# One-hot matrices of the first graph made on GpSimd, one behind each gather, in place of VectorE

## What is computed

```python
def _L0_gnn_ref(x, W, M, edge_src, edge_dst):
    self_term = x @ W
    msg = x @ M
    agg = jax.ops.segment_sum(msg[edge_src], edge_dst, num_segments=x.shape[0])
    return jax.nn.relu(self_term + agg)
...
x = x + _L0_gnn_ref(_layernorm(x, axis=-1), L0_gnn_W, L0_gnn_M, src, dst)
x = x + _L0_ffn_ref(_layernorm(x, axis=-1)[None], ...)[0]
```

## Time and profile before

| | us |
|---|---|
| median of 3 executions | 4055.15 |
| lowest, highest | 4053.32, 4062.95 |
| the profiled execution's own time | 4024.76 |
| its span, first to last instruction | 4023.5 |
| first gather of the visits starts | 63.84 |
| last gather of the visits starts | 2525.18 |

### The profile page before, as it was taken

The page is one execution under the profiler, slowest core; times in us unless marked ns, Lnnn a source line. Parts: engine busy times, 40 slices in busy tenths (PEclk is TensorE's granted clock), DMA queues, the critical chain, the costliest instruction groups (busy, mean ns, idle before and its releaser), DMA issues. The chain is left out here.

```text
span 4023.5 us, 43371 instructions
## 1 busy us (share of the span) xinstructions
PE 2676.5 (67%) x13459; PEld 1995.0 (50%) x13459; DVE 2157.3 (54%) x5820; ACT 903.1 (22%) x1563; POOL 2164.3 (54%) x2248
## 2 busy tenths in 40 slices
PE   2567867776677776877877877622694646555844
PEld 1344545554455455555555555401683535454844
DVE  6777667776655556554545555200263534344866
ACT  3001111111122221111111111100352423233633
POOL 4666666666666665666666666577014353534031
PEclk9767879898888888999899888755896867777978
DMA  9676656666666665666666666401221111111146
GB/s 298 207 253 189 195 182 201 202 195 190 191 202 198 194 191 173 206 204 199 209 195 208 209 202 194 112 13 14 64 70 27 45 27 32 39 26 36 44 138 203
DMA packets 476804, 601.22 MB, mean 149 GB/s; under 512 B 72486, under 2 KB 415390, under 8 KB 474526
## 3 DMA queue, kind: packets, MB, share of 16 engines
q1 hardware_dynamic: 378766, 375.94, 28.6%
q0 software_dynamic: 97216, 219.88, 20.0%
q10 hardware_dynamic: 592, 2.64, 0.2%
HBM read 313.06 MB, written 286.79 MB: 149 GB/s over the span
## 5 line engine op out<-in xcount | busy, mean ns | idle before, releaser
L1703 POOL DMA_INDIRECT ring<-xn_d,srci x1611 | 1567.2, 973 | 902.1 <-DVE ring L818 416.9
L1505 PE MATMUL wide<-ring,one_hot 128*128 128x256 f32 x3222 | 983.1, 442 | 470.5 <-DVE ring L818 351.7
L818 DVE SCALAR_TENSOR_TENSOR ring<-ring,same_v,wide 128x256 f32<-128x256 f32 x1610 | 770.3, 478 | 942.6 <-remote 405.9
L1505 PEld LDWEIGHTS wide<-ring,one_hot 128*128 128x128 f32 x3222 | 666.5, 218 | 740.8 <-DVE ring L818 318.4
L1611 PE MATMUL wide<-tab_parts,low_hot 128*128 128x208 bf16 x6288 | 659.9, 262 | 329.5 <-issue 308.7
L1737 POOL DMA_INDIRECT g<-tab_d,srt x500 | 480.8, 962 | 629.5 <-DMA sum_d<-g 480.4
L1611 PEld LDWEIGHTS wide<-tab_parts,low_hot 128*128 128x128 bf16 x6288 | 576.3, 100 | 413.2 <-issue 377.0
L1563 PE MATMUL wide<-w2s,hh 128*128 128x256 f32 x1568 | 424.8, 420 | 150.5 <-issue 88.5
L1563 PEld LDWEIGHTS wide<-w2s,hh 128*128 128x128 f32 x1568 | 335.5, 216 | 225.9 <-issue 102.8
L1553 PE MATMUL wide<-xt,w1s 128*128 128x512 f32 (+1 forms) x832 | 419.1, 631 | 41.2 <-ACT hh L1238 23.5
L1238 ACT ACTIVATE hh<-wide,b1c 128x512 f32<-128x512 f32 (+1 forms) x208 | 137.7, 663 | 1299.1 <-remote 627.3
(11 more groups left out here) (369 smaller groups left out, 1730.2 us busy)
## 6 DMA issues: line engine op xcount, KB each, us to landing
run_d<-ring SPq DMA_DIRECT2D x201, 1024.0 KB
ring<-xn_d,srci POOLq DMA_INDIRECT x1611
y_d<-yo SPq DMA_DIRECT2D x196, 128.0 KB
comb<-y_d SPq DMA_DIRECT2D x28, 896.0 KB, 10.5
low_row<-low_d SPq DMA_DIRECT2D x13, 1024.0 KB
sum_d<-g SPq DMA_DIRECT2D x15, 768.0 KB, 3.9
g<-tab_d,srt POOLq DMA_INDIRECT x500
xn_d<-ring SPq DMA_DIRECT2D x7, 896.0 KB, 7.0
```

The source lines that it names most:

```text
L818: dve_at["run", j] = step(V.scalar_tensor_tensor(out=o, in0=ring[:, (j - 1) // JC % RING, (j - 1) % JC, :], scalar=same_v[:, j:j + 1], in1 ...
L1505: T.matmul(wide[:, 4 + j // 2 % 2, j % 2 * D:(j % 2 + 1) * D], one_hot[:, j // 4 % 4, j % 4, :], ring[:, j // JC % RING, j % JC, :], start ...
L1703: G.indirect_dma_start(out=ring[:, s, j % JC, :], out_offset=None, in_=xn_d, in_offset=at_rows(srci[:, j:j + 1])).then_inc(sem(f"gather{s} ...
```

## The change

VectorE's one-hots (`visits_of`) are gone. POOL makes them instead with the same `tensor_scalar`, same operands, same size and same buffer of 16. It makes one for each visit, and each stands in POOL's order directly behind a gather: behind the gather of visit `j` the one-hot of visit `j - 6` (`HOT_LAG`). The last six follow the last gather. Before the first of them POOL waits for `same_v` on DVE (`same_tile`, with which `dloc` is complete); from visit 16 on, before each even one-hot, it waits until the matmuls that used its buffer are done (`visited`). PE waits for the one-hots of two visits at each even visit where it waited for four at each fourth.

```diff
@@ vector_program
-        step.settle()
+        dve_at["same_tile"] = step.settle()
...
-        def visits_of(b):
-
-            n = min(4, V_ - 4 * b)
-            for i in range(n):
-                dve_at["one_hot", b] = step(V.tensor_scalar(one_hot[:, b % 4, i, :], iota_f[:, :],
-                                                            dloc[:, 4 * b + i:4 * b + i + 1], None, ALU.is_equal))
...
-        visits_of(0)
-        visits_of(1)
...
-                if j % 4 == 0 and j + 8 < V_:
-                    visits_of(j // 4 + 2)
@@ tensor_program
         def visit(j):
-            if j % 4 == 0:
-                T.wait_ge(dve_step, dve_at["one_hot", j // 4])
+            if j % 2 == 0:
+                T.wait_ge(sem("one_hots"), min(j + 2, V_))
@@ gpsimd_program
+        def hot_rows(j):
+            if j % 2 == 0 and j >= 16:
+                G.wait_ge(sem("visited"), j - 14)
+            G.tensor_scalar(one_hot[:, j // 4 % 4, j % 4, :], iota_f[:, :], dloc[:, j:j + 1], None,
+                            ALU.is_equal).then_inc(sem("one_hots"), 1)
+
...
                 G.indirect_dma_start(out=ring[:, s, j % JC, :], out_offset=None, in_=xn_d,
                                      in_offset=at_rows(srci[:, j:j + 1])).then_inc(sem(f"gather{s}"), 16)
+                if j == HOT_LAG:
+                    G.wait_ge(dve_step, dve_at["same_tile"])
+                if j >= HOT_LAG:
+                    hot_rows(j - HOT_LAG)
+        for j in range(V_ - HOT_LAG, V_):
+            hot_rows(j)
```

More of the change, by code:

```diff
@@ L31 @@
 LEAD = 14
+HOT_LAG = 6
 TC = 32
```

## The result

The changed kernel takes 4638.53 us (median of 4) where the kernel before takes 4059.05 beside it: a ratio of 1.142, 95% interval 1.140 to 1.145. I had forecast 4150 with a range up to 4345. The sign was right, the size was not: 579 us lost in place of 95.

A forecast was written before the change was run, and what follows sets the result against it. The ring between PE and DVE bounded the kernel; with one-hots POOL would: 2486 us of visits + 25 hindered records + 45 waits = 2556 against 2461.3, so 4055.15 + 95 = 4150 us, range 3990 to 4345.

The forecast's parts named there:

- Who sets the pace now: Visits: the ring between PE and DVE sets 1.529 us a visit; POOL alone needs 1.253, leaving 0.275 us slack.
- What is added to POOL: One tensor_scalar behind each gather, priced at 0.29 us from the affine select's record, making POOL's visit 1.543 us.
- my upper bound: Highest price allowed for POOL's one-hot: 0.50 us, twice the affine select's spacing.
- my sum: Forecast stretch from first to last gather: 2486 + 25 + 45 = 2556 us against 2461.3, 95 us more.
- How it adds up with a gather: On POOL, a one-hot's full 0.29 us record adds to the gather's 1.253 us, the gather's 0.30 us gap remaining.
- Hindered records: Gathers and one-hots on POOL lengthened by DVE's instructions, such as the key sort: 25 us kept of 45.
- waits left: What POOL still waits for running sums beyond its lead of 14 visits: 45 us.
- What is removed from DVE: 1611 one-hots leave DVE, bounded by 0 and 354 us; 118 us taken as the PE and DVE ring's gain.
- A third: Share of DVE's one-hot time taken as gain for the ring of PE and DVE: 118 us.
- Rival 1: Faster: a one-hot adding under 0.275 us fits POOL's slack and DVE's relief counts; 3937 to 4035 us, chance 0.20.
- Rival 2: Much slower: POOL's one-hot costs 0.45 us, POOL never waits; 4363 us, chance 0.18 with all over 200 us slower.
- other estimate: By the skill's port rule, POOL one-hots meeting key sort minimum or maximum wait for its end: 45 us, not 25.

The follow-up runs named there:

- e2: Kernel before, VectorE keeping its one-hots, plus a spare unread one-hot on GpSimd behind each gather: 4029.24 us beside 3037.57 (1.327).
- e4: Changed so that GpSimd makes one one-hot in four and VectorE the others: 3270.09 us (1.076) where the kernel before takes 3038.
- g1: Kernel before with only 16 one-hots made on VectorE, which PE uses again, none on GpSimd: 4038.32 us beside 4059.18 (0.9953).
- e3: Kernel before with only 16 one-hots made on VectorE, which PE uses again, none on GpSimd: 3024.19 us beside 3037.57 (0.9955).
- h1: Kernel before, all one-hots on VectorE, plus a spare affine select on GpSimd behind each gather: 3983.39 us beside 4026.22 (0.990).
- h3: Kernel before, all one-hots on VectorE, plus a spare tensor_scalar on GpSimd behind each fourth gather: 3970.7 us beside 4026.22 (0.987).
- f3: Changed kernel with an affine select in place of GpSimd's one-hot tensor_scalar (matrices hold other values): 4008.1 us beside 4061.59 (0.987).
- g3: Changed so that GpSimd makes one one-hot in two and VectorE the others: 4158.17 us (1.025) where the kernel before takes 4059.
- e1: Kernel before plus ten groups of four extra GpSimd instructions at its start, to price each form: the one-hot's form starts 0.59 us apart.
- h4: Kernel before with GpSimd's lead over the running sums cut from 14 visits to 10: 4392.58 us beside 4026.22 (1.092).

## Why the prediction was wrong

- **Who sets the pace now.** Right for the chip of the comparison: GpSimd had about 0.275 us a visit of slack there. It is a fact of the chip, though, not of the kernel: on another it has at most 0.06 (1.311 - 1.253), and there e2 paid the whole price of its instruction and e4 233 of 247 us.
- **What is added to POOL: the step that failed.** "The nearest row is the affine select of the same size ... I take the record, 0.29 us." The instruction adds 0.61 us between two gathers (1.866 - 1.253), over my upper bound of 0.50. Same size, same types and one tensor input did not make the row near: on GpSimd the affine select and the copy start 0.25 and 0.23 us apart, `tensor_scalar` 0.49, and the column of scalars adds 0.09. The error is 1611 x 0.32 = 520 us. With 42 more for hindered records and 45 less for waits (below) it makes the 517 us by which the traced stretch exceeded my sum; between the medians the miss is 484 us.
- **How it adds up with a gather.** Also wrong, the other way: I said that a record behind a gather counts in full. The affine select counts 0.17 of its 0.30 us there. Had I taken the right row's spacing, 0.59, its sum with 1.253 would have been 1.84, right within 0.03.
- **Hindered records, 25 us; waits left, 45 us.** Measured 67 and 0. At 1.87 us a visit GpSimd waits for nobody.
- **What is removed from DVE, 118 us.** 21 us by g1, 13 by e3. "A third" had no row behind it. The 994 us in which VectorE waited anyway were in front of me and said nearly nothing.
- **The cost of a loaded GpSimd under the threshold.** I took it as nothing at best. At 1.41 us a visit it is a gain of 40 to 55 us on the chips at 4020 to 4060 (h1, h3), and with 0.17 us in place of 0.61 the whole change would have been one (f3, 4008). Rival 1's threshold of 0.275 us was thus rightly placed (0.153 and 0.17 us a visit gain, 0.307 in g3 costs 99 us), though the gain under it is not the one I gave, VectorE's relief.
- **Rivals.** Rival 2 was the mechanism (GpSimd never waits, PE stands for gathers and one-hots), its price (0.45) still too low. The waits of the change, its first and its last six one-hots cost nothing that the trace shows, as said; everything behind the visits is as long as before, as said. The Trainium skill's rule ("GPSIMD Engine Reference", section "3. Performance versus the Vector engine") that VectorE is about twice as fast, which I set beside the sum at an estimated 0.44 us, pointed to the right side; the traces give 0.59 us (e1) against 0.22, a factor of 2.7.
- **Contention.** The key sort's instructions on VectorE went from 566 ns to 591 and 589, and a one-hot can take 0.87 us (at 623.97 us) where it takes 0.63. In the changed kernel's trace 147 one-hots overlap a minimum or maximum of the key sort, and together they are 50 us longer than 0.63 us each. That is most of the 67 us, and near the 45 us that the prediction had as its other estimate for these one-hots.

## What to carry to other kernels

Before moving an instruction to GpSimd, measure that very form: the opcode, whether it takes a column of scalars, and its width. Start-to-start distance in a chain of four tells it in one run, and no other opcode's row stands in for it. Add it to the busiest queue's own cycle (here 1.25 us of a gather and its gap), not to the share of its busy time. And relief of an engine that waits for another is worth nothing until a run without the work says so.

## What the runs showed that I had not expected

- The 0.30 us between two indirect DMAs on GpSimd is partly free for other work: an affine select of 0.30 us in it costs 0.17 (f3).
- Useless work on GpSimd made the kernel before 1.0 to 1.3% faster on a chip where PE is held back (h1, h3). The fastest there is the lead of 18 with a spare instruction behind each fourth gather, 3962.54 us (0.985, 0.984 to 0.987), which beats both kernels; of the kernels that put the instruction to use it is one one-hot in four on GpSimd, 4005.03. Neither is a version to keep without knowing the chip: the latter cost 7.6% where before takes 3038.
- Four visits less of lead (10 in place of 14) cost 366 us, four more (18) gave nothing. PE begins a chunk only when its eight gathers are in. With a lead of 10 GpSimd waits 872.2 us for running sums (the page of h4), where before has 416.9.
- The same kernel took 3038 us in one comparison and 4020 to 4062 in all others. In the visits the records of VectorE and of GpSimd's gathers have the same length on both kinds of chip; PE is held back on the one.
